# Cross-attention on one core: scores by pair of heads, each head's scores in two matmuls of 32 by 64

## The chip, the cores and the metric

The kernel runs on one core of a Trainium2 chip. The metric is the device time of one execution in microseconds (us); the median of several runs counts. Engines are named as in the profile: PE is TensorE's matmuls, PEld its weight loads, DVE is VectorE, ACT is ScalarE, POOL is GpSimd, SP is SyncE, whose queue issues the DMAs.

## What is computed

A block of cross-attention with 16 heads of 32, all in float32, over 4096 queries and 3202 keys of width 512:

```python
xq = _ada_ln(x_q, t_vec, Wss_q, bss_q)
xkv = _ada_ln(x_kv, t_vec, Wss_kv, bss_kv)
q = (xq @ Wq + bq).reshape(B, Lq, nh, dh)
kv = (xkv @ Wkv + bkv).reshape(B, Lkv, 2, nh, dh)
k = kv[:, :, 0]
v = kv[:, :, 1]
scores = jnp.einsum('bqhd,bkhd->bhqk', q, k) / jnp.sqrt(jnp.float32(dh))
attn = jax.nn.softmax(scores, axis=-1)
out = jnp.einsum('bhqk,bkhd->bqhd', attn, v).reshape(B, Lq, H)
return x_q + (out @ Wp + bp)
```

`_ada_ln` is a layer norm with a scale and a bias computed from the condition vector.

## The kernel before

The first 230 us compute keys and values and store them to device memory, and the queries of the first block. Then the attention runs in 32 units: unit `u` is one block of 512 queries (`b = u // 4`, eight blocks) and one group of four heads (`g = u % 4`). Four heads of 32 fill the 128 partitions: `rows_of(h)` is the 32 partitions of head `h`. A unit goes through its keys in 25 steps of 128 (`t`, `NT = 25`); the last two keys are done apart ("tail").

Each step has four parts, by four engines' own hand-written order:

- `scores(u, t)` (L641 to L660, matmul at L658), on PE: for each of the four heads a matmul with 32 rows of contraction and 128 columns of keys, 512 queries wide, into a PSUM bank of its own. The banks form a ring of `RING = 3` pairs: item `n` (a pair of heads in a step; `items(u) + 2 t + pair`) uses banks `2 (n % 3)` and the next.
- `weights(u, t)` (L890 to L904), on ACT: two exponentials, one per pair of heads, each from two banks into `pt[t % 5]`. Each signals `e_done` once.
- `weigh(u, t)` (L662 to L672, matmul at L670), on PE: four matmuls of 128 rows and 32 columns, the values times the weights, adding up in bank 6 or 7. It waits for both exponentials of its step.
- an addition of 128x2048 on DVE (L1175, L1182), which sums the weights over the steps. It waits for both exponentials of its step.

PE's order is `scores(t + 1)`, `weigh(t)`, then a side job of step `t`, if there is one (`first_side`, `later_side`, L752 to L787): four matmuls of 128 rows and 32 columns that project the next block's queries (L700), multiply by the output matrix for the block before (L746), sum the denominators (L711), the tail (L682, L732), or four transposes (L722). ACT copies what such jobs produce out of PSUM between its exponentials. The order is written out by hand; no scheduler is involved. The waits are counts on semaphores: `e_done` counts exponentials, `s_ready` counts score groups, `pv_done` counts weightings (it frees `pt`), `p_added` counts additions. The wait of `scores` on `e_done` to be `n - 1` is for the first exponential of the step before.

Of the kernel before, what the change touches and what calls it, by code (L numbers as in the profile page):

```python
# [5 lines left out]
P = 128  # L6
# [15 lines left out]
def cross_attention(nc, x, ctx, cond, Wq, bq, Wkv, bkv, Wp, bp, Wss_q, bss_q, Wss_kv, bss_kv, out):  # L22
# [4 lines left out]
    HG = P // DH  # L27
# [5 lines left out]
    NT = LKV // P  # L33
# [4 lines left out]
    RING = 3  # L38
# [32 lines left out]
    def rows_of(h):  # L71
        return slice(h * DH, (h + 1) * DH)
# [4 lines left out]
    def attention():  # L77
        with ExitStack() as st:
            def sb(name, shape, dt=F32):
                return st.enter_context(nc.sbuf_tensor(name, shape, dt))  # L80

            def sem(name):
                return st.enter_context(nc.semaphore(name))
# [4 lines left out]
            qs = sb("qs", [P, NG, QB])  # L88
            xt = sb("xt", [P, FT, QB])
            xin = sb("xin", [P, TPB, H])  # L90
            ks = sb("ks", [P, NT * P])
# [63 lines left out]
            bank = st.enter_context(nc.psum_tensor("bank", [P, 8, 512], F32))  # L155
# [33 lines left out]
            s_ready = sem("s_ready")  # L189
            e_done = sem("e_done")  # L190
# [84 lines left out]
            def side_bank(u):  # L275
                return 7 - u % 2

            def add_of(t):
                return max(t - 1, 1) if t < 2 or t > 3 else 2

            def items(u):
                return 2 * NT * u
# [7 lines left out]
            with nc.Block() as block:  # L290
# [255 lines left out]
                def _(pe):  # L546
# [94 lines left out]
                    def scores(u, t):  # L641

                        g = u % NG
                        n = items(u) + 2 * t
                        if u == 0 and t == 0:
                            pe.wait_ge(xt_ready, FT * N_SEQ)
                            pe.wait_ge(kq_taken, KQ_JOBS)
                        if u == 0 and t == 1:
                            pe.wait_ge(v_taken, V_JOBS)
                        if t == 0 and u >= NG:  # L650
                            pe.wait_ge(job_taken, JOB["q", u // NG, g, 1] + 1)
                        if t % CT == 0:
                            pe.wait_ge(k_in[t // CT], 32 * (u + 1))
                        if n > 0:
                            pe.wait_ge(e_done, n - 1)
                        for h in range(HG):
                            i = n + h // 2
                            mm = nc.tensor.matmul(bank[:, 2 * (i % RING) + h % 2, :], ks[rows_of(h), t * P:(t + 1) * P],  # L658
                                                  qs[rows_of(h), g, :], start=True, stop=True)
                        mm.then_inc(s_ready, 1)  # L660

                    def weigh(u, t):  # L662

# [124 lines left out]

                    pe.wait_ge(fills, 1)
                    scores(0, 0)  # L790
                    for u in range(UNITS):
                        b, g = divmod(u, NG)
                        for t in range(NT):
                            if t + 1 < NT:
                                scores(u, t + 1)
                            elif u + 1 < UNITS:
                                scores(u + 1, 0)
                            weigh(u, t)
                            if g == 0:
                                first_side(u, b, t)  # L800
                            else:
                                later_side(u, b, g, t)
# [16 lines left out]
                    for h in range(HG):  # L819
                        nc.tensor.matmul(bank[rows_of(h), side_bank(UNITS), :], ones[:, :], acc[(UNITS - 1) % 2][:, h, :],  # L820
                                         start=True, stop=False, skip_group_check=True)
                    for h in range(HG):
                        mm = nc.tensor.matmul(bank[rows_of(h), side_bank(UNITS), :], ones_blk[:, h, :], p_tail[:, :],
                                              start=False, stop=True, skip_group_check=True)
# [12 lines left out]
                def _(act):  # L837
# [52 lines left out]
                    def weights(u, t):  # L890

                        b, g = divmod(u, NG)
                        if NT * u + t - PR >= 0:
                            act.wait_ge(pv_done, NT * u + t - PR + 1)
                            if t < PR:
                                act.wait_ge(p_added, ADDS * (u - 1) + add_of(t + NT - PR))
                            else:
                                act.wait_ge(p_added, ADDS * u + add_of(t - PR))
                        for pair in range(2):
                            n = items(u) + 2 * t + pair  # L900
                            first = 2 * (n % RING)
                            act.wait_ge(s_ready, NT * u + t + 1)
                            nc.scalar.activation(pt[t % PR][:, 2 * pair:2 * pair + 2, :], bank[:, first:first + 2, :],  # L903
                                                 ACT.Exp, scale=SCALE, bias=shift[:, g:g + 1]).then_inc(e_done, 1)  # L904

# [42 lines left out]
                    for u in range(UNITS):  # L948
                        b, g = divmod(u, NG)
                        for t in range(NT):  # L950
                            weights(u, t)
                            if t == 0 and u > 0:
                                take_sums(u - 1)
# [724 lines left out]
```

## Time and profile before

| | us |
|---|---|
| median of 3 runs | 2272.64 |
| lowest, highest | 2270.13, 2272.66 |
| the profiled execution | 2269.04 |
| its span, first to last instruction | 2267.3 |
| PE busy | 2181.9 |
| DVE busy | 1902.1 |
| ACT busy | 1822.7 |

All durations below are from the one profiled execution. A matmul in float32 leaves two records of PE and two of PEld, one for each of its two passes. A record's start is when it was taken up; the end of a matmul is modelled, so that groups that follow one another overlap in the records, and distances between starts say more than busy times. A row of the timeline merges neighbours of one kind: its first number is the start of the first, its second is the time to the end of the last, and the number behind the `x` says how many records are in it. What stands in brackets is how long the engine was idle before, and who ended that.

### The profile page before, as it was taken

How to read it: one execution, taken by the hardware profiler on the slowest of the kernel's cores; microseconds unless marked ns; L12 is line 12 of the kernel's file. 1: busy time of each engine (PE TensorE's matmuls, PEld its weight loads, DVE VectorE, ACT ScalarE, POOL GpSimd, SP SyncE). 2: the span in 40 equal slices, each digit the busy share in tenths (PEclk: the TensorE clock that was granted, in tenths of full speed). 3: DMA queues.
4: the chain of work that ended last, by engine and by line, in shares of the span. 5: the costliest groups of instructions: out<-in, count | busy, mean ns of one | idle time of the engine just before them, and what ended most of it. 6: DMA issues, size and time to landing. Idle time of an engine off the chain costs nothing.

```text
span 2267.3 us, 43846 instructions
## 1 busy us (share of the span) xinstructions
PE 2181.9 (96%) x18978; PEld 675.0 (30%) x18978; DVE 1902.1 (84%) x1095; ACT 1822.7 (80%) x1908; POOL 29.7 (1%) x29
## 2 busy tenths in 40 slices
PE   7999899999999999999999999999999999999997
PEld 3444222223222222222222222222222222222222
DVE  2322789989999899989998999989998998889887
ACT  1211888889888988898888888898888988888884
POOL 0000000000000000000000000000000000000000
PEclk9999999999999999999999999999999999999999
DMA  7232222224222322223121422132212321232111
GB/s 285 100 121 97 77 59 54 62 61 119 63 62 68 112 64 57 69 69 115 57 69 57 120 65 64 57 98 82 69 57 69 93 73 57 64 97 64 54 43 56
DMA packets 171384, 180.10 MB, mean 79 GB/s; under 512 B 14000, under 2 KB 117168, under 8 KB 171184
## 3 DMA queue, kind: packets, MB, share of 16 engines
q1 hardware_dynamic: 171184, 177.22, 26.3%
q8 instruction: 151, 2.47, 0.5%
q14 instruction: 49, 0.40, 0.1%
HBM read 146.27 MB, written 30.92 MB: 78 GB/s over the span
## 4 chain that ended last, share of the span: by engine, by line
PE 89%; ACT 7%; issue 2%; DMA 1%; DVE 1%; ACTq 0%; SPq 0%; POOL 0%; DVEq 0%
PE bank L658 38%; PE bank L670 29%; ACT arena L903 6%; PE bank L593 4%; PE bank L700 4%; PE bank L746 4%; PE bank L605 4%; PE bank L711 1%; PE bank L682 1%; PE bank L574 1%; PE bank L808 1%; PE bank L722 1%; DMA arena<-in_ctx_dram 0%; DMA arena<-l_recip 0%; PE bank L732 0%
## 5 line engine op out<-in xcount | busy, mean ns | idle before, releaser
L903 ACT ACTIVATE arena<-bank,shift 128x1024 f32<-128x1024 f32 x1600 | 1695.5, 1112 | 230.7 <-PE bank L658 218.9
L1175 DVE TENSOR_TENSOR arena<-arena 128x2048 f32<-128x2048 f32 x736 | 1676.4, 2289 | 175.9 <-ACT arena L903 175.0
L658 PE MATMUL bank<-qs,ks 32*128 32x512 f32 x6400 | 912.3, 639 | 54.3 <-ACT arena L903 40.0
L670 PE MATMUL bank<-arena,vg 128*32 128x512 f32 x6400 | 852.3, 605 | 1.3 <-ACT arena L903 1.3
L658 PEld LDWEIGHTS bank<-qs,ks 32*128 32x128 f32 x6400 | 254.4, 183 | 412.8 <-ACT arena L903 305.6
L670 PEld LDWEIGHTS bank<-arena,vg 128*32 128x32 f32 x6400 | 125.9, 108 | 608.3 <-ACT arena L903 607.5
L746 PE MATMUL bank<-wp,arena 128*32 128x168 f32 (+2 forms) x2464 | 153.7, 321 | 0.8 <-DVE arena L1108 0.8
L700 PE MATMUL bank<-xt,wq 128*32 128x256 f32 x1792 | 137.7, 379 | 0.0
L746 PEld LDWEIGHTS bank<-wp,arena 128*32 128x32 f32 x2464 | 80.0, 110 | 185.6 <-issue 171.0
L1053 DVE TENSOR_TENSOR arena<-bank,bv_b 128x512 f32<-128x512 f32 (+1 forms) x26 | 17.9, 690 | 128.8 <-PE bank L605 128.6
L867 ACT ACTIVATE arena<-bank,bk_c 128x512 f32<-128x512 f32 (+1 forms) x28 | 18.0, 642 | 133.6 <-PE bank L593 133.6
L700 PEld LDWEIGHTS bank<-xt,wq 128*32 128x32 f32 x1792 | 58.2, 110 | 134.1 <-issue 123.6
L605 PE MATMUL bank<-arena 128*128 128x512 f32 (+1 forms) x208 | 93.6, 592 | 0.0
L593 PE MATMUL bank<-arena 128*128 128x512 f32 (+1 forms) x224 | 90.8, 549 | 1.1 <-ACT arena L850 1.1
L1182 DVE TENSOR_TENSOR arena<-arena 128x2048 f32<-128x2048 f32 x32 | 73.3, 2292 | 1.1
L593 PEld LDWEIGHTS bank<-arena 128*128 128x128 f32 x224 | 39.7, 190 | 45.3 <-issue 43.8
L605 PEld LDWEIGHTS bank<-arena 128*128 128x128 f32 (+1 forms) x208 | 38.4, 186 | 49.1 <-issue 48.9
L524 POOL TENSOR_TENSOR rstd<-var_eps,minus_half 128x4 f32<-128x4 f32 x15 | 27.1, 1805 | 1574.7 <-DVE var_eps L1012 1574.7
L850 ACT ACTIVATE arena<-bank,mod 128x512 f32<-128x512 f32 (+1 forms) x28 | 18.8, 745 | 33.3 <-PE bank L574 33.2
L682 PE MATMUL bank<-p_tail,vt 128*32 128x256 f32 x512 | 39.3, 379 | 0.0
L711 PE MATMUL bank<-arena,ones 128*32 128x256 f32 x496 | 38.1, 379 | 0.0
L682 PEld LDWEIGHTS bank<-p_tail,vt 128*32 128x32 f32 x512 | 16.6, 110 | 38.3 <-issue 29.9
(86 smaller groups left out, 428.1 us busy)
## 6 DMA issues: line engine op xcount, KB each, us to landing
ks<-k_full SPq DMA_DIRECT2D x160, 320.0 KB, 3.1
vg<-v_full SPq DMA_DIRECT2D x160, 320.0 KB, 3.7
xin<-in_x_dram SPq DMA_DIRECT2D x8, 1024.0 KB, 9.7
q_full<-qs SPq DMA_DIRECT2D x32, 256.0 KB, 2.1
arena<-in_x_dram SPq DMA_DIRECT2D x8, 1024.0 KB, 10.0
out_dram<-arena SPq DMA_DIRECT2D x32, 256.0 KB, 2.0
arena<-l_recip SPq DMA_DIRECT2D x28, 256.0 KB, 5.9
arena<-in_ctx_dram SPq DMA_DIRECT2D x6, 1024.0 KB, 7.9
```

The lines of the kernel that those rows point to most:

```text
L524: nc.gpsimd.tensor_tensor(rstd[:, :], var_eps[:, :], minus_half[:, :], ALU.pow).then_inc(rstd_ready, 1)
L593: mm = nc.tensor.matmul(bank[:, 4 + 2 * (n % 2), 0:width], w[:, k, m * P:(m + 1) * P], src[:, k, 0:width], start=(k == 0), stop=(k == FT - 1))
L605: mm = nc.tensor.matmul(bank[0:rows, 5 + 2 * (n % 2), :], ct[c % 2][:, k, j * P:j * P + rows], wkv[:, k, H:2 * H], start=(k == 0), stop=(k ...
L658: mm = nc.tensor.matmul(bank[:, 2 * (i % RING) + h % 2, :], ks[rows_of(h), t * P:(t + 1) * P], qs[rows_of(h), g, :], start=True, stop=True)
L670: mm = nc.tensor.matmul(bank[rows_of(h), o_bank(u), :], vg[:, t, rows_of(h)], pt[t % PR][:, h, :], start=(t == 0), stop=False, skip_group_ ...
L682: mm = nc.tensor.matmul(bank[rows_of(h), o_bank(u), cols], vt[:, g, rows_of(h)], p_tail[:, cols], start=False, stop=True, skip_group_check ...
L700: mm = nc.tensor.matmul(bank[rows_of(c), side_bank(u), halves_of(half)], wq[:, k, col:col + DH], xt[:, k, halves_of(half)], start=(k == 0) ...
L711: mm = nc.tensor.matmul(bank[rows_of(h), side_bank(u), halves_of(half)], ones[:, :], acc[of % 2][:, h, halves_of(half)], start=True, stop= ...
L746: mm = nc.tensor.matmul(bank[rows_of(c), side_bank(u), cols], on[:, k, row:row + DH], wp[:, k, cols], start=(k == 0), stop=(k == NG - 1), ...
L903: nc.scalar.activation(pt[t % PR][:, 2 * pair:2 * pair + 2, :], bank[:, first:first + 2, :], ACT.Exp, scale=SCALE, bias=shift[:, g:g + 1]) ...
L1175: nc.vector.tensor_tensor(a[:, :, :], (pt[t - 1] if k <= 2 else a)[:, :, :], pt[t % PR][:, :, :], ALU.add).then_inc(p_added, 1)
L1182: nc.vector.tensor_tensor(sums[0][:, :, :], sums[0][:, :, :], acc2[:, :, :], ALU.add).then_inc(p_added, 1)
```

## The change

In `scores`, the four matmuls of a step become two groups, one per pair of heads. Each group has its own wait on `e_done`, for the exponentials that last read its own pair of banks (`i - RING + 1`), and its own signal on `s_ready`. Each head's matmul of 32 by 128 becomes two of 32 by 64: one for the first 64 keys, whose scores go to partitions 0 to 63 of the bank, and one for the other 64. So a group has four matmuls. On ACT, each exponential waits for its own pair's count.

```diff
-                        if n > 0:
-                            pe.wait_ge(e_done, n - 1)
-                        for h in range(HG):
-                            i = n + h // 2
-                            mm = nc.tensor.matmul(bank[:, 2 * (i % RING) + h % 2, :], ks[rows_of(h), t * P:(t + 1) * P],
-                                                  qs[rows_of(h), g, :], start=True, stop=True)
-                        mm.then_inc(s_ready, 1)
+                        for pair in range(2):
+                            i = n + pair
+                            if i >= RING:
+                                pe.wait_ge(e_done, i - RING + 1)
+                            for side in range(2):
+                                out = slice(side * P // 2, (side + 1) * P // 2)
+                                keys = slice(t * P + side * P // 2, t * P + (side + 1) * P // 2)
+                                for h in (2 * pair, 2 * pair + 1):
+                                    mm = nc.tensor.matmul(bank[out, 2 * (i % RING) + h % 2, :], ks[rows_of(h), keys],
+                                                          qs[rows_of(h), g, :], start=True, stop=True)
+                            mm.then_inc(s_ready, 1)
...
-                            act.wait_ge(s_ready, NT * u + t + 1)
+                            act.wait_ge(s_ready, n + 1)
```

The first pair's wait is for item `n - 3`, the second exponential of the step before the last one; the second pair's is for item `n - 2`, the first exponential of the step before, which is what the whole group waited for.

PE's order in two steps with the side job L746, before (names are out<-in, sizes are partitions by elements of the output; L658 is the scores, L670 the weighting):

```order
L746 MATMUL bank<-wp,arena 32x168 [waits on_ready,job_taken]
L746 MATMUL bank<-wp,arena 32x168 x3
L658 MATMUL bank<-qs,ks 128x512 [waits e_done]
L658 MATMUL bank<-qs,ks 128x512 x3
L670 MATMUL bank<-arena,vg 32x512 [waits e_done]
L670 MATMUL bank<-arena,vg 32x512 x3
```

The same place of the changed kernel, whose lines stand four lower (L662 is the scores, L674 the weighting, L750 the side job):

```order
L750 MATMUL bank<-wp,arena 32x168 [waits on_ready,job_taken]
L750 MATMUL bank<-wp,arena 32x168 x3
L662 MATMUL bank<-qs,ks 64x512 [waits e_done]
L662 MATMUL bank<-qs,ks 64x512 x3
L662 MATMUL bank<-qs,ks 64x512 [waits e_done]
L662 MATMUL bank<-qs,ks 64x512 x3
L674 MATMUL bank<-arena,vg 32x512 [waits e_done]
L674 MATMUL bank<-arena,vg 32x512 x3
```

One group of four scores with one wait has become two groups of four with a wait each; the side job ahead and the weighting behind stand where they stood.

PE's order in a step with the side job L700, before:

```order
L700 MATMUL bank<-xt,wq 32x256 [waits job_taken]
L700 MATMUL bank<-xt,wq 32x256 x3
L658 MATMUL bank<-qs,ks 128x512 [waits e_done]
L658 MATMUL bank<-qs,ks 128x512 x3
L670 MATMUL bank<-arena,vg 32x512 [waits e_done]
L670 MATMUL bank<-arena,vg 32x512 x3
L700 MATMUL bank<-xt,wq 32x256 x4
```

The same place of the changed kernel, where L700 is L704:

```order
L704 MATMUL bank<-xt,wq 32x256 [waits job_taken]
L704 MATMUL bank<-xt,wq 32x256 x3
L662 MATMUL bank<-qs,ks 64x512 [waits e_done]
L662 MATMUL bank<-qs,ks 64x512 x3
L662 MATMUL bank<-qs,ks 64x512 [waits e_done]
L662 MATMUL bank<-qs,ks 64x512 x3
L674 MATMUL bank<-arena,vg 32x512 [waits e_done]
L674 MATMUL bank<-arena,vg 32x512 x3
L704 MATMUL bank<-xt,wq 32x256 x4
```

Here too the scores alone differ. On the other engines nothing moves.

## Rows read from the trace of the kernel before

**Rows 1.** The page: span, busy times, 40 slices, and the additions of VectorE.
```profile
span 2267.3 us, 43846 instructions
PE 2181.9 (96%) x18978; PEld 675.0 (30%) x18978; DVE 1902.1 (84%) x1095; ACT 1822.7 (80%) x1908; POOL 29.7 (1%) x29
...
PEclk9999999999999999999999999999999999999999
...
L1175 DVE TENSOR_TENSOR arena<-arena 128x2048 f32<-128x2048 f32 x736 | 1676.4, 2289 | 175.9 <-ACT arena L903 175.0
```

**Rows 2.** The page: the chain that ended last, by engine and by line.
```profile
PE 89%; ACT 7%; issue 2%; DMA 1%; DVE 1%; ACTq 0%; SPq 0%; POOL 0%; DVEq 0%
PE bank L658 38%; PE bank L670 29%; ACT arena L903 6%; PE bank L593 4%; PE bank L700 4%; PE bank L746 4%; PE bank L605 4%; PE bank L711 1%; PE bank L682 1%; PE bank L574 1%; PE bank L808 1%; PE bank L722 1%; DMA arena<-in_ctx_dram 0%; DMA arena<-l_recip 0%; PE bank L732 0%
```

**Rows 3.** The waits: us in total, times, longest.
```profile
PEld bank L658 <- ACT arena L903: 305.6, 625, 1.2
ACT arena L903 <- PE bank L658: 218.9, 607, 1.4
```

**Rows 4.** The timeline of steps with L746, in us from the start.
```profile
1201.10 1.14 PE L658 MATMUL bank<-qs,ks 32*128 32x512 f32 x8
1202.17 1.07 PE L670 MATMUL bank<-arena,vg 128*32 128x512 f32 x8
1202.39 2.12 ACT L903 ACTIVATE arena<-bank,shift 128x1024 f32<-128x1024 f32 x2 [0.34 <-PE bank L658]
1203.06 0.47 PE L746 MATMUL bank<-wp,arena 128*32 128x168 f32 x8
1203.57 1.14 PE L658 MATMUL bank<-qs,ks 32*128 32x512 f32 x8
...
1202.39 1.12 ACT L903 ACTIVATE arena<-bank,shift 128x1024 f32<-128x1024 f32 x1 [0.34 <-PE bank L658]
...
1203.20 0.33 PE L746 MATMUL bank<-wp,arena 128*32 128x168 f32 x4
...
1204.86 2.12 ACT L903 ACTIVATE arena<-bank,shift 128x1024 f32<-128x1024 f32 x2 [0.34 <-PE bank L658]
```

**Rows 5.** The timeline of a step with L700, on PE.
```profile
902.34 1.14 PE L658 MATMUL bank<-qs,ks 32*128 32x512 f32 x8
...
904.29 0.61 PE L700 MATMUL bank<-xt,wq 128*32 128x256 f32 x8
...
904.50 0.40 PE L700 MATMUL bank<-xt,wq 128*32 128x256 f32 x4
...
904.83 0.71 PE L658 MATMUL bank<-qs,ks 32*128 32x512 f32 x4
```

**Rows 6.** The timeline of a step without a side job.
```profile
298.10 1.14 PE L658 MATMUL bank<-qs,ks 32*128 32x512 f32 x8 [0.32 <-ACT arena L903]
299.08 2.29 DVE L1175 TENSOR_TENSOR arena<-arena 128x2048 f32<-128x2048 f32 x1 [0.43 <-ACT arena L903]
...
300.56 1.14 PE L658 MATMUL bank<-qs,ks 32*128 32x512 f32 x8 [0.32 <-ACT arena L903]
```

**Rows 7.** Groups of matmuls by line, from 230 to 2240 us: records and times.
```profile
L658 PE MATMUL bank<-qs,ks 32*128 32x512 f32 x6400 | 912.3, 639 | 54.3 <-ACT arena L903 40.0 <-ACT arena L867 0.7
...
L746 PE MATMUL bank<-wp,arena 128*32 128x168 f32 (+2 forms) x2464 | 153.7, 321 | 0.8 <-DVE arena L1108 0.8
L700 PE MATMUL bank<-xt,wq 128*32 128x256 f32 x1792 | 137.7, 379 | 0.0
L682 PE MATMUL bank<-p_tail,vt 128*32 128x256 f32 x512 | 39.3, 379 | 0.0
L711 PE MATMUL bank<-arena,ones 128*32 128x256 f32 x496 | 38.1, 379 | 0.0
L722 PE MATMUL bank<-ident,xin 128*128 128x128 f32 x112 | 18.4, 286 | 0.0
L732 PE MATMUL bank<-qs,kt 128*32 128x512 f32 x64 | 8.3, 592 | 0.0
```

**Rows 8.** First and second passes in narrow windows; durations of L658, min/median/max.
```profile
1203.57 0.71 PE L658 MATMUL bank<-qs,ks 32*128 32x512 f32 x4
...
1204.10 0.61 PE L658 MATMUL bank<-qs,ks 32*128 32x512 f32 x4
1204.64 0.64 PE L670 MATMUL bank<-arena,vg 128*32 128x512 f32 x4
...
1205.09 0.61 PE L670 MATMUL bank<-arena,vg 128*32 128x512 f32 x4
...
L658 PE MATMUL bank<-qs,ks x6400: 587/625/692, 230.3 to 2235.0; 32*128 32x512 f32 x194
```

**Rows 9.** Busy time of each engine over unit 10.
```profile
core 0: us, PE busy (x) PEld busy (x) DVE busy (x) ACT busy (x) POOL busy (x), PEclk, DMA share, GB/s
857.60:919.90 62.30, 61.26 (x592) 18.08 (x593) 57.70 (x31) 55.01 (x58) 2.99 (x1) 1.00 0.22 63
```

**Rows 10.** The same view: a step with L746, and a burst (L615 alone).
```profile
1201.10:1203.56 2.46, 2.42 (x24) 0.73 (x24) 2.29 (x2) 2.12 (x3) 0.00 (x0) 1.00 0.31 91
...
101.50:102.80 1.30, 1.17 (x32) 1.01 (x32) 1.00 0.38 129
```

## The prediction

> **What bounds the kernel now.** I read the page first. TensorE is busy for 96% of the 2267.3 us span, VectorE 84%, ScalarE 80%, and the clock is at its full level in all 40 slices [rows 1]. The chain that ended last is 89% TensorE and 7% ScalarE; the score matmuls are 38% of it and the weighting matmuls 29% [rows 2]. That looks like a kernel bound by TensorE alone, but the ends of matmuls are modelled, so I look for what sets the start of each group. Two rows say that ScalarE is in the loop too: it sat idle 218.9 us in 607 places for the scores of L658, and the weight loads of L658 waited 305.6 us in 625 places for ScalarE's exponentials [rows 3]. Two engines that wait for each other are a loop of latencies.
>
> The loop can be read off one step of 128 keys (a "step" from here; 25 a unit, 32 units, 800 in all) [rows 4]. ScalarE starts the exponentials of the first pair of heads at 1202.39 and needs 1.12, so to 1203.51. The next scores start at 1203.57, 0.05 later. Their group takes 1.14, to 1204.71, and ScalarE starts again at 1204.86, 0.15 later. 1.12 + 0.05 + 1.14 + 0.15 = 2.46, which is the step (1203.57 - 1201.10 = 2.47, 1204.86 - 1202.39 = 2.47).
>
> Would TensorE alone be faster there? From the start of the scores to that of the weighting it is 1.07 (1202.17 - 1201.10), from there to the side job 0.89 (1203.06 - 1202.17). The side job's two passes are 0.14 apart (1203.06, 1203.20), so it streams for 0.28. What lies between its end and the next scores when nothing is waited for is to be had from a step with a longer side job: L700 starts at 904.29, its second pass at 904.50, so it streams 0.42, and the scores start at 904.83, 0.12 after that [rows 5]. So TensorE needs 1.07 + 0.89 + 0.28 + 0.12 = 2.36 in a step with L746, and has 0.10 to spare. In a step with L700 it needs 2.50 (904.83 - 902.34 = 2.49), over the loop's 2.46: there TensorE is the bound. A step without a side job takes 2.46 too (300.56 - 298.10), though TensorE needs 1.07 + 0.89 + 0.12 = 2.08 [rows 6].
>
> The kinds are counted by their records, eight to a step: L746 2464 / 8 = 308 steps, bound by the loop; L700 1792 / 8 = 224, L682 and L711 (both 128x256) 126, L722 and L732 some 36, together 386 bound by TensorE; the other 800 - 694 = 106 have no side job and are bound by the loop [rows 7].
>
> **The change, part by part.** *The waits.* Before, all four score matmuls of a step wait until the first pair of exponentials of the step before is done. After, the first pair (items i, i-3) waits for exponentials that ended long before, one pair earlier; only the second pair waits for what all waited for. ScalarE's first exponential now waits for the first pair's scores alone. So the loop goes over two steps: first pair of scores, ScalarE, second pair of scores of the next step, weighting, side job, first pair again. Behind TensorE's new wait stand the second pair and all that follows it; ScalarE and VectorE wait for that only through the weighting and the pt buffers, of which there are five.
>
> *The weight loads.* The two passes of the scores start 0.53 apart (1203.57, 1204.10), those of the weighting 0.45 (1204.64, 1205.09) [rows 8]. The loads differ by 128 - 32 = 96 columns, so 0.08 / 96 us a column is exposed ahead of a group's first pass; the second pass's load is hidden. 64 columns in place of 128 expose 0.05 less.
>
> *The number of matmuls.* Eight in place of four, so 16 records a step more. The first passes of four tiles of 32 by 128 start together, four records before 1203.7 and the other four from 1204.10 on [rows 8]: four tiles stream at once, each reading a 512-wide row block. No row shows tiles of 32 by 64. From below: if all eight stream at once, the cost is the stagger. The four first passes cover 0.71 where one lasts 692 ns, the four second ones 0.61 where one lasts 587 ns [rows 8], so four starts lie within 0.02, and four more add 0.02 to 0.03. From above: if the second four start only when the first four have gone to their second pass, the second pair lags 0.53 - 0.05 = 0.48. If 32 by 64 halves the rate of streaming, it is 2 x 0.43 = 0.85. I take the lower end, because tiles that share row groups (L670, 128 by 32) and tiles that share columns (L658, 32 by 128) each run four at once in these rows, and the two halves of a head share only rows.
>
> *The sum.* In a step with L746 the new loop is: first pair start, +1.14 - 0.05 scores, +0.15, +1.12 exponentials, +0.05: the second pair of the next step starts at 2.41. Then 1.07 - 0.05 = 1.02, 0.89, 0.28 and 0.12 to the first pair of the step after: 4.72, for two steps, so 2.36. TensorE's own need is 2.36 - 0.05 + 0.03 = 2.34. The step goes from 2.46 to 2.36: 308 x 0.10 = 31 us. Where TensorE is the bound, only load against stagger is left, 0.03: 386 x 0.03 = 11 us, taken as 10. Without a side job the loop gives (2.41 + 1.02 + 0.89 + 0.12) / 2 = 2.22, but VectorE's add takes 2.29 [rows 1, 6] and then is late next: with 2.30 it is 106 x 0.16 = 17 us. ScalarE's two exponentials are 2.12 [rows 4], no bound. Over a unit VectorE is busy 57.70 of 62.30 us and ScalarE 55.01 [rows 9]; the unit would become 60.3, so both stay just under it. Start and end of the kernel are untouched.
>
> 31 + 10 + 17 = 58. The profiled execution took 2269.04, so 2211; the median of the runs is 3.6 above that execution, so **2214 us**.
>
> **What could go otherwise.** *Slower: the second pair queues behind the first's second pass.* Every matmul of the program leaves two records (4 x 800 = 3200 matmuls, 6400 records [rows 7]). If a pass can't go ahead of an older one that still waits for its tile, beyond the four that the rows show, the second pair lags 0.48. The scores then need 0.48 + 1.02 = 1.50 where they needed 1.07: 386 x 0.43 = 166, with L746 a step of 1.50 + 0.89 + 0.40 = 2.79, 308 x 0.33 = 102, without a side job 2.51, 106 x 0.05 = 5; 273 us in all, so 2546 for the median. The point from which the change costs: a lag l with 386 (l - 0.03) + 308 (l - 0.10) = 17, so l = 0.09 us. For it speaks that no row has more than four first passes in flight; against it that the four first passes in rows 8 are within 0.02 of each other although, in the program, the second pass of head 0 stands ahead of the first pass of head 1: a waiting pass doesn't hold up other tiles there.
>
> [...]
>
> *Slower: half the rate, or TensorE's issue.* At half rate 386 x 0.80 + 308 x 0.72 + 106 x 0.42 = 575, so 2848. Issue: steps now hold 64 records in 2.36 us, 37 ns each, where the trace sustains 48 in 2.46, 51 ns, and only in a burst 64 in 1.17 us, 18 ns [rows 10]. Had the issue no reserve at 51 ns, steps with a side job would take 64 x 51 ns = 3.26, some 694 x 0.78 = 541 us more in all; the burst speaks against it.
>
> *Smaller: the first pair is not signalled earlier.* If the first pair's last pass ends, as ScalarE sees it, only with the second pair's, the old loop stays with a shorter load: 0.05 + 1.09 + 0.15 + 1.12 = 2.41. That saves 0.05 x 414 + 10 = 31, so 2242. Near it lies a gain cut by ScalarE's own side work (seven or so of 25 steps have one), which delays the exponential that the second pair waits for.
>
> **How the numbers follow.** All tiles at once and the loop broken: 0.70, between 2190 and 2235. Smaller gain or none, 2235 to 2272: 0.10. Second pair queued, about 2546: 0.15. Half rate or issue, over 2700: 0.05. The range from 2183 to 2270 holds the first two, some 0.8; its low end is TensorE's own need without any lag (308 x 0.12 + 386 x 0.05 + 106 x 0.24 = 82 us, and the rounding of the steps). A measurement of this kernel tells about 0.2% (4.5 us) from no change: faster 0.78, same 0.03, slower 0.19.
>
> **What would show it.** In the timeline of a step with L746, right if: the first score matmuls start 0.12 after the side job's last pass has streamed; eight first passes start within 0.1 us; ScalarE's idle time per step shrinks from 0.34 to about 0.24; the step is 2.36, and one with L700 2.46. The idle time of L658's loads for ScalarE should fall from 305.6 us on the first pair and appear, much smaller, on the second. Wrong if: first passes of the second pair start 0.45 or more after those of the first though ScalarE was done (queued), if passes are 0.9 apart (half rate), or if ScalarE's first exponential starts 0.15 after the second pair's end (signal). VectorE's idle 175.9 us before L1175 [rows 1] should shrink by about what the kernel gains.

## The result, and the profile after

The changed kernel takes 2204.39 us (median of 4 runs, 2203.38 to 2204.53) against 2272.14 us: a ratio of 0.9702, 95% interval 0.9686 to 0.9719, so 3.0% faster. The forecast was 2214 us, in a range of 2183 to 2270.

The page of the changed kernel: span, busy times, the chain that ended last by engine, and the two groups whose idle time mattered, with the scores between them. L907 is the exponentials, L1179 VectorE's additions, L662 the scores (L903, L1175 and L658 before).

```profile
span 2202.5 us, 56645 instructions
PE 2167.0 (98%) x25378; PEld 628.5 (29%) x25378; DVE 1895.3 (86%) x1095; ACT 1820.7 (83%) x1908; POOL 29.7 (1%) x29
...
PE 96%; DMA 2%; DVE 1%; issue 1%; ACT 0%; SPq 0%; POOL 0%
...
L907 ACT ACTIVATE arena<-bank,shift 128x1024 f32<-128x1024 f32 x1600 | 1692.2, 1113 | 162.7 <-PE bank L662 156.0
L1179 DVE TENSOR_TENSOR arena<-arena 128x2048 f32<-128x2048 f32 x736 | 1670.0, 2289 | 113.6 <-ACT arena L907 100.8
L662 PE MATMUL bank<-qs,ks 32*64 32x512 f32 x12800 | 922.2, 613 | 1.1 <-ACT arena L871 0.7
```

No duration of any other engine changed; idle time did. ScalarE waited 156.0 us for scores where it had waited 218.9 [rows 3], VectorE was idle 113.6 us where it had been 175.9 [rows 1], and ScalarE's 7% of the chain [rows 2] is 0%. TensorE is 96% of the chain now. That share alone shows no bound, since it was 89% when the loop was the bound. The starts of the groups below say more: TensorE sets the pace of the steps with L704, and in the steps with the output job or without a side job the loop over two steps still costs a few hundredths.

The timeline of steps with the output job (the product with the output matrix, L750; L746 before), the counterpart of [rows 4] and [rows 8]. The rows of 8 records of L662 and of 4 records of L750 are of narrow windows, which separate the passes:

```profile
865.23 1.11 PE L662 MATMUL bank<-qs,ks 32*64 32x512 f32 x16
...
865.23 0.69 PE L662 MATMUL bank<-qs,ks 32*64 32x512 f32 x8
...
865.71 0.63 PE L662 MATMUL bank<-qs,ks 32*64 32x512 f32 x8
...
866.28 1.06 PE L674 MATMUL bank<-arena,vg 128*32 128x512 f32 x8
...
867.30 0.33 PE L750 MATMUL bank<-wp,arena 128*32 128x168 f32 x4
867.56 0.74 PE L662 MATMUL bank<-qs,ks 32*64 32x512 f32 x8
...
867.56 1.17 PE L662 MATMUL bank<-qs,ks 32*64 32x512 f32 x16
...
869.93 1.11 PE L662 MATMUL bank<-qs,ks 32*64 32x512 f32 x16
...
864.09 2.12 ACT L907 ACTIVATE arena<-bank,shift 128x1024 f32<-128x1024 f32 x2 [0.21 <-PE bank L662]
866.47 2.12 ACT L907 ACTIVATE arena<-bank,shift 128x1024 f32<-128x1024 f32 x2 [0.26 <-PE bank L662]
868.79 2.12 ACT L907 ACTIVATE arena<-bank,shift 128x1024 f32<-128x1024 f32 x2 [0.21 <-PE bank L662]
```

All eight first passes are inside 0.69 us, and one lasts 638 ns at most (duration view, below), so they start within 0.05 of one another: both pairs stream at once. The eight second passes start from 865.71 on, 0.48 after the first ones. ScalarE's two-step distance is 868.79 - 864.09 = 4.70, where two steps took 4.92 before. Its idle time is 0.21 and 0.26 in turn, where it was 0.34. TensorE's steps take turns too, 2.33 (867.56 - 865.23) and 2.37 (869.93 - 867.56): in the second one the group spans 1.17 in place of 1.11, because the second pair still waits a little for ScalarE.

A step with L704 (L700 before), the counterpart of [rows 5]:

```profile
879.82 1.11 PE L662 MATMUL bank<-qs,ks 32*64 32x512 f32 x16
880.87 1.07 PE L674 MATMUL bank<-arena,vg 128*32 128x512 f32 x8
881.75 0.61 PE L704 MATMUL bank<-xt,wq 128*32 128x256 f32 x8
...
881.96 0.40 PE L704 MATMUL bank<-xt,wq 128*32 128x256 f32 x4
882.29 0.68 PE L662 MATMUL bank<-qs,ks 32*64 32x512 f32 x8
```

It takes 882.29 - 879.82 = 2.47 where it took 2.49. And steps without a side job, the counterpart of [rows 6]:

```profile
297.88 1.11 PE L662 MATMUL bank<-qs,ks 32*64 32x512 f32 x16
298.93 1.07 PE L674 MATMUL bank<-arena,vg 128*32 128x512 f32 x8
299.92 1.45 PE L662 MATMUL bank<-qs,ks 32*64 32x512 f32 x16
301.30 1.06 PE L674 MATMUL bank<-arena,vg 128*32 128x512 f32 x8
302.30 1.11 PE L662 MATMUL bank<-qs,ks 32*64 32x512 f32 x16
```

Steps of 2.04 and 2.38 take turns, where each took 2.46. In the longer one the two pairs are apart: the group spans 1.45 in place of 1.11, because the second pair waits 0.34 for ScalarE while the first already streams.

Where the 65 us of the span came from. This is line L662 in the duration view (min/median/max in ns, then first and last start), against L658's 230.3 and 2235.0 in [rows 8]:

```profile
L662 PE MATMUL bank<-qs,ks x12800: 587/588/638, 233.1 to 2167.7; 32*64 32x512 f32 x197
```

From first to last score matmul it is 1934.6 us where it was 2004.7: the steps gave 70.1. The prologue was 2.8 longer in this execution (its code is untouched, and it ends between 230.5 and 233.5 in the executions below), and the end after the last scores 2.5 longer: 34.8 in place of 32.3. By kind, from the starts of all groups (mean step before and after): the 308 with the output job 2.495 and 2.390, together 32 us; the 224 with L700 2.506 and 2.472, 8 us; the 106 without a side job 2.488 and 2.169, 34 us; the 63 with the tail (L682) 2.506 and 2.598, 6 us the other way; the rest 2 us. Against the shorter steps shown above, 2.33 with the output job and 2.04 without a side job, the loop still costs an estimated 308 x 0.06 + 106 x 0.13 = 32 us.

### The profile page after: what moved, and what is told of

The parts are those of the page before. It is cut to its first block, busy times and chain, and to the rows that moved or that the text cites. A ratio compares the mean times of both kernels' runs of the same rounds, so it can differ in the third digit from the quotient of the medians.

```text
span 2202.5 us, 56645 instructions
## 1 busy us (share of the span) xinstructions
PE 2167.0 (98%) x25378; PEld 628.5 (29%) x25378; DVE 1895.3 (86%) x1095; ACT 1820.7 (83%) x1908; POOL 29.7 (1%) x29
## 4 chain that ended last, share of the span: by engine, by line
PE 96%; DMA 2%; DVE 1%; issue 1%; ACT 0%; SPq 0%; POOL 0%
PE bank L662 38%; PE bank L674 35%; PE bank L593 5%; PE bank L750 4%; PE bank L704 4%; PE bank L605 4%; PE bank L715 1%; PE bank L686 1%; DMA arena<-l_recip 1%; PE bank L574 1%; PE bank L812 1%; PE bank L726 1%; DMA arena<-in_ctx_dram 0%; DVE arena L1112 0%; DMA l_recip<-r_blk 0%
## 5 line engine op out<-in xcount | busy, mean ns | idle before, releaser
L907 ACT ACTIVATE arena<-bank,shift 128x1024 f32<-128x1024 f32 x1600 | 1692.2, 1113 | 162.7 <-PE bank L662 156.0
L1179 DVE TENSOR_TENSOR arena<-arena 128x2048 f32<-128x2048 f32 x736 | 1670.0, 2289 | 113.6 <-ACT arena L907 100.8
L662 PE MATMUL bank<-qs,ks 32*64 32x512 f32 x12800 | 922.2, 613 | 1.1 <-ACT arena L871 0.7
L674 PE MATMUL bank<-arena,vg 128*32 128x512 f32 x6400 | 852.3, 605 | 1.3 <-ACT arena L907 1.3
L674 PEld LDWEIGHTS bank<-arena,vg 128*32 128x32 f32 x6400 | 125.9, 108 | 650.6 <-ACT arena L907 648.2
L662 PEld LDWEIGHTS bank<-qs,ks 32*64 32x64 f32 x12800 | 206.8, 129 | 346.8 <-ACT arena L907 204.5
L750 PE MATMUL bank<-wp,arena 128*32 128x168 f32 (+2 forms) x2464 | 153.7, 321 | 1.7 <-DVE arena L1112 1.7
L704 PE MATMUL bank<-xt,wq 128*32 128x256 f32 x1792 | 137.7, 379 | 0.0
L750 PEld LDWEIGHTS bank<-wp,arena 128*32 128x32 f32 x2464 | 79.9, 110 | 186.8 <-issue 170.2
L704 PEld LDWEIGHTS bank<-xt,wq 128*32 128x32 f32 x1792 | 58.2, 110 | 134.1 <-issue 120.0
```

The lines of the kernel that those rows point to most:

```text
L662: mm = nc.tensor.matmul(bank[out, 2 * (i % RING) + h % 2, :], ks[rows_of(h), keys], qs[rows_of(h), g, :], start=True, stop=True)
L674: mm = nc.tensor.matmul(bank[rows_of(h), o_bank(u), :], vg[:, t, rows_of(h)], pt[t % PR][:, h, :], start=(t == 0), stop=False, skip_group_ ...
L704: mm = nc.tensor.matmul(bank[rows_of(c), side_bank(u), halves_of(half)], wq[:, k, col:col + DH], xt[:, k, halves_of(half)], start=(k == 0) ...
L750: mm = nc.tensor.matmul(bank[rows_of(c), side_bank(u), cols], on[:, k, row:row + DH], wp[:, k, cols], start=(k == 0), stop=(k == NG - 1), ...
L1179: nc.vector.tensor_tensor(a[:, :, :], (pt[t - 1] if k <= 2 else a)[:, :, :], pt[t % PR][:, :, :], ALU.add).then_inc(p_added, 1)
```

## The experiments

My theory: before, the step was a loop of latencies between TensorE and ScalarE, and the change makes the loop span two steps; the shorter weight load adds 0.05 us a step, less the stagger of four more matmuls. The rivals: the shorter load is the gain and the waits were hidden; one of the two semaphores does it alone; VectorE takes over as the bound; TensorE holds only so many tiles. Ratios are to the kernel before, with 95% intervals.

### One part at a time

**Pairs alone.** The change's waits and signals, with each head's scores in one matmul:

```diff
-                            for side in range(2):
-                                out = slice(side * P // 2, (side + 1) * P // 2)
-                                keys = slice(t * P + side * P // 2, t * P + (side + 1) * P // 2)
-                                for h in (2 * pair, 2 * pair + 1):
-                                    mm = nc.tensor.matmul(bank[out, 2 * (i % RING) + h % 2, :], ks[rows_of(h), keys],
+                            for h in (2 * pair, 2 * pair + 1):
+                                mm = nc.tensor.matmul(bank[:, 2 * (i % RING) + h % 2, :], ks[rows_of(h), t * P:(t + 1) * P],
```

> The waits and signals by pair of heads alone; each head's scores stay one matmul of 32 by 128. Theory (a loop over two steps): a step with the side job L746 takes (2.45 + 1.07 + 0.89 + 0.40) / 2 = 2.41 us where before has 2.46 and the change 2.36; steps with a side job of 256 columns stay at 2.50; steps without a side job (2.45 + 2.08) / 2 = 2.27. 308 x 0.05 + 106 x 0.22 = 39 us off: about 2233 us. Rival (the shorter weight load is what gains, the waits are hidden anyway): as before, 2272 us.

Measured: 2224.11 us, ratio 0.9795 (0.9778 to 0.9811), 48 us off. The steps with the output job are 2.414 in the mean (median 2.410), those with a side job of 256 columns (L700 and L711) 2.50, as expected; those without a side job 2.20 and not 2.27, which is most of the 9 us by which it beat the forecast. So the waits and signals are the larger part, and the rival falls. The narrower matmuls bring the other 20 us on top of them: with them the steps with the output job go from 2.414 to 2.390, those with L700 from 2.499 to 2.472.

**Halves alone.** The two matmuls a head, with one wait and one signal:

```diff
+                        if n > 0:
+                            pe.wait_ge(e_done, n - 1)
                         for pair in range(2):
                             i = n + pair
-                            if i >= RING:
-                                pe.wait_ge(e_done, i - RING + 1)
...
-                            mm.then_inc(s_ready, 1)
+                        mm.then_inc(s_ready, 1)
...
-                            act.wait_ge(s_ready, n + 1)
+                            act.wait_ge(s_ready, NT * u + t + 1)
```

> The matmuls of 32 by 64 alone; all eight wait together, as in the kernel before, and one signal stands behind the eighth. Theory: the loop of before stays, with a load shorter by 0.05 and a stagger longer by 0.03 us: 2.44 us a step with L746 or without a side job, 2.47 with 256 columns. 414 x 0.02 to 0.03 + 386 x 0.03 = 20 us off: about 2252 us. Rival (the shorter load is what gains): 2204 us, as the change.

Measured: 2269.9 us (10 runs), ratio 0.999 (0.998 to 0.9999): next to nothing, where I expected 20 us. The rival falls further still, but the theory missed too. The timeline of this kernel, a step with the output job (L750):

```profile
1203.11 0.47 PE L750 MATMUL bank<-wp,arena 128*32 128x168 f32 x8
1203.64 1.12 PE L662 MATMUL bank<-qs,ks 32*64 32x512 f32 x16
1204.69 1.07 PE L674 MATMUL bank<-arena,vg 128*32 128x512 f32 x8
1204.95 1.11 ACT L907 ACTIVATE arena<-bank,shift 128x1024 f32<-128x1024 f32 x1 [0.35 <-PE bank L662]
```

The weighting starts 1.05 after the scores, 0.02 earlier than before, as expected. But ScalarE starts 1204.95 - 1203.64 = 1.31 after them, where it was 1204.86 - 1203.57 = 1.29 before [rows 4]. The load is 0.05 shorter, and yet ScalarE starts later: by this estimate (0.02 + 0.05) four more matmuls ahead of the signal cost 0.07 and not the 0.03 by which the records are staggered. So the loop is 2.47 in place of 2.46, and the steps with the output job lose 3.5 us in all (mean 2.495 before, 2.506 now); those with L700 win 4 (2.506 and 2.490). All steps together win 2 us.

**Sixteen tiles.** As the change, with four matmuls of 32 columns a head (`range(4)` and `P // 4` in place of `range(2)` and `P // 2`).

> As the change, but each head's scores are four matmuls of 32 by 32 columns: sixteen tiles a step, 96 records. Theory (all tiles stream at once; a column of load exposes 0.08/96 us, a tile costs a stagger of 0.007 us): load 0.03 less, stagger 0.05 more, so steps bound by TensorE 2.50, those with L746 2.37: 386 x 0.03 + 308 x 0.01 = 14 us more than the change, about 2218 us. Rival (TensorE holds only so many waiting passes, or its issue is near its end at eight tiles): the second pair's first passes start 0.4 us or more after the first pair's, over 2450 us.

Measured: 2230.49 us, ratio 0.9818 (0.9801 to 0.9834), 26 us over the change where 14 were expected. Its timeline, with L704:

```profile
1200.97 1.16 PE L662 MATMUL bank<-qs,ks 32*32 32x512 f32 x32
1202.06 1.06 PE L674 MATMUL bank<-arena,vg 128*32 128x512 f32 x8
1202.24 2.12 ACT L907 ACTIVATE arena<-bank,shift 128x1024 f32<-128x1024 f32 x2 [0.40 <-PE bank L662]
```

Thirty-two records are done in 1.16 where sixteen took 1.11, and all sixteen first passes start within 0.12. So sixteen tiles with two passes each stream at once here, and TensorE neither holds back the second pair nor runs out of issue: the two slow rivals of the prediction are out with margin. The price is a little over what I gave it: the weighting starts 1.09 after the scores, 0.04 later than in the change (1.05), where load and stagger were to make 0.02. Part of that is in the stagger: in this step fourteen first passes start 0.007 apart, the last two 0.015 and 0.018. Sixty-four columns are the better size.

### Which semaphore does it

**One signal.** As the change, with its waits by pair; the edit is the last two pieces of the diff above.

> As the change, but ScalarE gets one signal, behind the second pair's last matmul, and starts its first exponential by it. Theory: exponential of the first pair, second pair of scores, signal, exponential is a loop in one step: 1.12 + 0.05 + 1.09 + 0.15 = 2.41 us, for steps with L746 and for those without a side job: 308 x 0.05 + 106 x 0.25 = 43 us more than the change, about 2247 us. Rival (the first pair's earlier start is what counts, its signal is not): 2204 us.

Measured: 2233.83 us, ratio 0.9834 (0.9818 to 0.9851). Steps with the output job have a median of 2.406, as the loop says (mean 2.427); those without a side job average 2.287 and not 2.41, about the 13 us by which the whole is below the forecast. Their median is 2.403, but some 30 of them take 2.04; why these escape the loop stays open.

**One wait.** As the change, with its signals by pair; the edit is the first two pieces of that diff.

> As the change, but all eight score matmuls wait together, as before, for the first exponential of the step before; each pair still has its own signal. Theory: exponential, first pair of scores, exponential is a loop within one step again: 1.12 + 0.05 + 1.09 + 0.15 = 2.41 us with L746 or without a side job, 2.47 with 256 columns. About what one signal with two waits gave, 2234 us, between 2228 and 2247. Rivals: the early signal alone is the gain, 2204 us; the early wait alone is, 2270 us, as the halves alone.

Measured: 2238.87 us, ratio 0.9858 (0.9842 to 0.9875), inside the range; the steps with the output job have a median of 2.413 (mean 2.444), and those without a side job average 2.435. Halves alone, with neither, is at 2270 us. The early wait takes 36 us off that, the early signal 31, and both together, the change, 66: each takes its own piece out of the loop, and the two add up. Neither rival, that one of them does it all, holds.

**A later wait.** As the change, with the second pair waiting for one exponential more:

```diff
-                                pe.wait_ge(e_done, i - RING + 1)
+                                pe.wait_ge(e_done, i - RING + 1 + pair)
```

> As the change, but the second pair waits for one exponential more, the second of the step before. Theory: the loop over two steps is longer by one exponential, about 1.00 us (1203.41 - 1202.39 = 1.02 between the starts of two): 2.41 + 1.00 = 3.41 to the second pair; with L746 (3.41 + 1.02 + 0.89 + 0.40) / 2 = 2.86 us a step, with 256 columns 2.93, without a side job 2.72. 308 x 0.50 + 386 x 0.46 + 106 x 0.5 = 385 us more than the change, about 2590 us. Rival (TensorE has the time hidden under the weighting, only the first pair's wait counts): under 2250 us.

Measured: 2572.1 us, ratio 1.1323 (1.1301 to 1.1346); 368 us over the change where 385 were expected. Steps average 2.871 with the output job (2.86 expected), 2.927 with L704 (2.93), 2.68 without a side job (2.72). Single steps with the output job run from 2.33 to 3.38, but two of them in a row mostly take 5.71, where the formula of the two-step loop gives 5.72. So the formula holds with a term made 1.00 us longer, to 0.01 where there is a side job, and the rival, under 2250, falls. Its timeline:

```profile
1202.02 1.74 PE L662 MATMUL bank<-qs,ks 32*64 32x512 f32 x16
1203.26 2.12 ACT L907 ACTIVATE arena<-bank,shift 128x1024 f32<-128x1024 f32 x2 [0.63 <-PE bank L662]
1203.69 1.06 PE L674 MATMUL bank<-arena,vg 128*32 128x512 f32 x8
```

The group spans 1.74: the second pair starts 0.63 later than in the change (1.74 - 1.11), ScalarE is idle for 0.63, and the weighting starts 1.67 after the scores and not 1.05. This is also what the slow rival of the prediction would have looked like: a second pair that lags costs TensorE the whole of its lag.

### Is VectorE the bound now?

**Half additions.** From the third addition of a unit on, VectorE adds two of four heads:

```diff
-                            nc.vector.tensor_tensor(a[:, :, :], (pt[t - 1] if k <= 2 else a)[:, :, :], pt[t % PR][:, :, :],
+                            few = HG if k <= 2 else 2
+                            nc.vector.tensor_tensor(a[:, 0:few, :], (pt[t - 1] if k <= 2 else a)[:, 0:few, :],
```

> As the change, but from the third addition of a unit on VectorE adds two of the four heads (128x1024 in place of 128x2048), so the denominators of the others are wrong. Theory: VectorE is nowhere the bound of the changed kernel; its lateness is taken up by the five pt buffers: within 3 us of the change, 2204. Rival (the addition's 2.29 us is the floor of steps without a side job and of unit ends): 10 us or more below it.

Measured: 2197.47 us, ratio 0.9678 (0.9662 to 0.9694), 7 us below the change: between the two forecasts. The same unit in both kernels, busy times by engine (PE, PEld, DVE, ACT, POOL); first the change, then half additions:

```profile
833.90:894.20 60.30, 60.30 (x796) 16.49 (x792) 57.72 (x36) 55.09 (x58) 2.99 (x1) 1.00 0.23 65
```

```profile
833.90:894.20 60.30, 60.30 (x800) 16.48 (x795) 35.04 (x30) 55.08 (x58) 0.00 (x0) 1.00 0.23 65
...
L662 PE MATMUL bank<-qs,ks x12800: 587/588/638, 230.7 to 2163.5; 32*64 32x512 f32 x197
```

VectorE does 35.04 us in place of 57.72 and the unit is as long, with TensorE busy all of it. From first to last score matmul it is 1932.8, against 1934.6: the steps gave 1.8 us. Another 2.4 are the prologue of this execution, which the edit doesn't touch, and 3.1 lie behind the last scores (31.7 in place of 34.8), where VectorE's last additions are waited for. So VectorE bounds no step; it costs at the end alone.

## Why the prediction was right, and where it was off

**What bounds the kernel.** Right: a loop of 2.46 between two engines of which neither was full. That each of the two semaphores is worth about half, and that a longer wait lengthens the two-step loop by the predicted amount, is shown by the runs.

**The steps with the output job.** Forecast 31 us from 2.46 to 2.36; measured 32 us, 4.70 for two steps in a row. The means are 2.495 and 2.390: both are 0.03 above the step that the forecast was read from, so the difference holds.

**The steps bound by TensorE.** Forecast 0.03 a step, 10 us in all; those with L700 gained 0.034. Those with the tail lost 0.09 in the mean. They stand at the end of a unit beside a step without a side job, which now starts early, so part of that one's gain is given back in the next: at most ends of a unit the two take 2.04 and 2.81 where they took 2.55 and 2.50, 0.20 less together. The loss goes with the waits by pair: with one wait these steps average 2.487, with pairs alone 2.627. VectorE is not its cause, for half additions leave 2.598. What makes the second of the two so long stays open; the steps of both kinds together are the better number.

**The steps without a side job.** This was the term that was mis-sized: 17 us forecast, 34 measured, 28 after what the tail steps lost. The step that failed is that "VectorE's add takes 2.29" and "then is late next". Two errors are in it. Additions that follow one another start 2.20 apart, not 2.29; three of them in a row, in the change:

```profile
891.71 6.69 DVE L1179 TENSOR_TENSOR arena<-arena 128x2048 f32<-128x2048 f32 x3
```

(6.69 - 2.29) / 2 = 2.20. And a unit has 24 additions for 25 steps, with five pt buffers between ScalarE and VectorE, so that it is VectorE's average over a unit that counts, not the single step. In a run of such steps the loop I had worked out and set aside, 2.22, is what came: (302.30 - 297.88) / 2 = 2.21. Where one stands alone between longer steps it takes 2.04, TensorE's own need, because the loop is over two steps and its neighbour pays. Half additions confirm that VectorE was no bound.

**Eight tiles at once.** I took the lower end of the cost, and the runs bear that out up to sixteen tiles. In the slow rival the second pair was to lag 0.48. The trace of the change shows no such lag: all eight first passes start within 0.05, and the first of the second passes 0.43 after the last of them. In the program the second pair's wait and its matmuls stand behind all of the first pair's, and yet their first passes start before the first pair's second passes.

**The stagger.** I took 0.02 to 0.03 for four more matmuls from the records, which holds for the weighting that follows (1.05 after the scores and not 1.07). It does not hold for the signal, and the change escapes that because each of its signals stands behind four matmuls, as many as before. Here the sum was right for a reason it had not stated: halves alone, where eight stand ahead of the signal, won nothing.

**The ends.** Start and end were called untouched. The end is 2.5 us longer: VectorE, whose slack has gone, starts its last addition 10.0 us after the last scores (2177.74 against 2167.7), where it was 8.0 (2243.00 against 2235.0). What the change gains on VectorE's wait is in part handed back there.

```profile
2177.74 2.29 DVE L1186 TENSOR_TENSOR arena<-arena 128x2048 f32<-128x2048 f32 x1
```

```profile
2243.00 2.29 DVE L1182 TENSOR_TENSOR arena<-arena 128x2048 f32<-128x2048 f32 x1
```

The sum, 58, stands against 65 in the span: 17 more from steps without a side job, 6 less from those with the tail, 1 more with the output job, 5 less at both ends. The medians are 68 apart, 3 more than the spans: the forecast added the 3.6 by which the profiled execution before lay below the median, and the profiled execution after, 2204.24, lies only 0.15 below its own.

**The signs.** The first scores start 0.12 after the output job has streamed (867.30 + 0.14, 867.56), as foretold, and ScalarE's idle time, the two-step distance and the step with L704 came within 0.03. VectorE's idle time fell by 62 us, where the span fell by 65. One sign did not come: the idle time of the scores' weight loads for ScalarE fell from 305.6 us only to 204.5, in 527 places, and some 194 of it still lies ahead of the first pair. It was a poor sign, for this view books time to ScalarE also in steps that TensorE bounds, as here behind L704, where the step is 2.47:

```profile
872.40 0.23 PEld L662 LDWEIGHTS bank<-qs,ks 32*64 32x64 f32 x16 [0.41 <-ACT arena L907]
```

So the 305.6 us of [rows 3] say less than they seemed to; what carries the argument is the loop read from the starts.

## What to carry to other kernels

When two engines are both busy for 80 to 98% and yet wait for each other in most rounds, add up one round of latencies, signals included, before believing that either of them is the bound: here the loop, 2.46 us, hid 0.10 us of TensorE's reserve in every step with the output job. To break such a loop, split the group so that its first part neither waits for the newest result nor signals with the last part; each of the two gave about half (36 and 31 us of 66). The floor that a third engine sets is to be estimated from its average over the buffers between, not from the duration of one of its instructions: here VectorE's additions take 2.29 us each and 57.72 in a unit of 60.30, and steps of 2.04 and 2.38 took turns beside them.

## What the runs showed of the hardware

- The score matmuls in float32, of 32 rows by 64 columns in the change and by 32 in sixteen tiles, stream eight and sixteen at once: the eight first passes from 865.23 on start within 0.05 us, the sixteen from 1200.97 on within 0.12, both ahead of any second pass, and 32 records are done in 1.16 us where 16 take 1.11.
- A matmul ahead of a semaphore's signal costs an estimated 0.017 us in these runs, more than the 0.007 by which records are staggered ((0.69 - 0.638) / 7 in the change). From the start of a group to the exponential that it releases: two matmuls of 128 columns 1.25 (pairs alone, 1201.34 - 1200.09), four of 128 1.29 (before), four of 64 1.24 (the change, 866.47 - 865.23), eight of 64 1.31 (halves alone), eight of 32 1.27 (sixteen tiles, two groups of eight). With the estimate of 0.0008 us a column of load (0.08 / 96), these agree within 0.01 with one price of 0.017 a matmul.

The two rows of pairs alone, on PE and ACT:

```profile
1200.09 1.14 PE L659 MATMUL bank<-qs,ks 32*128 32x512 f32 x8
...
1201.34 2.12 ACT L904 ACTIVATE arena<-bank,shift 128x1024 f32<-128x1024 f32 x2 [0.38 <-PE bank L659]
```

- The columns of the weight load show only in the first pass of the score matmuls in these traces: a first pass's record lasts 692 ns with 128 columns and 638 with 64, a second pass's 587 with either; the passes start 0.53 apart with 128 columns [rows 8], 0.48 with 64 (865.71 - 865.23) and 0.45 with the 32 of the weighting [rows 8]. So 64 columns in place of 128 gave 0.05 us, as the difference between 128 and 32 had said.
